# One read for both blocks of a pair, and PSUM banks split between pairs and scores, in the second layer's attentions

## The chip, the cores and the metric

The kernel runs on 1 core of a Trainium2 chip. The metric is the device time of one execution, in microseconds (us). Engines: PE is TensorE (PEld its weight loads), DVE is VectorE, ACT is ScalarE, POOL is GpSimd, SP is SyncE, which issues most DMAs.

## The reference

Two transformer layers over x (4 batches, 512 tokens, 256 features) with a context of 4 x 1601 x 192. Layer 0 has heads of 64, layer 1 has 16 heads of 16; each layer holds a self attention, a cross attention on the context and feed-forward blocks. The part that matters here is layer 1:

```python
def _attn(x, ctx, wq, wk, wv, wo, bo, num_heads):
    q = (x @ wq).reshape(B, T, num_heads, hd)      # hd = 16
    k = (ctx @ wk).reshape(B, S, num_heads, hd)
    v = (ctx @ wv).reshape(B, S, num_heads, hd)
    scores = jnp.einsum('bthd,bshd->bhts', q, k) / np.sqrt(hd)
    p = jax.nn.softmax(scores, axis=-1)
    o = jnp.einsum('bhts,bshd->bthd', p, v).reshape(B, T, E)
    return o @ wo + bo
x = _attn(_ln(x, n1_g, n1_b), _ln(x, n1_g, n1_b), sq_w, sk_w, sv_w, so_w, so_b, 16) + x
x = _ffn(_ln(x, n2_g, n2_b), f1_w1, f1_b1, f1_w2, f1_b2) + x
x = _attn(_ln(x, n3_g, n3_b), context, cq_w, ck_w, cv_w, co_w, co_b, 16) + x
x = _ffn(_ln(x, n4_g, n4_b), f2_w1, f2_b1, f2_w2, f2_b2) + x
```

## The kernel before

`build` runs five stretches one after the other. The two attentions of the second layer, `a2` (SELF1, 512 keys) and `a3` (CROSS1, 1601 keys), are both written by `attend_narrow`, each followed by its projections and feed-forward. Only that function changes.

**Groups and units.** Four heads of one batch are a group; there are 16 groups. A group's keys come in chunks of 128: 4 chunks in a2, 13 in a3. One chunk of one group is a unit, numbered tau. A group's softmax needs each query row's maximum before its exponentials, so the scores are computed twice: once in the other orientation only for the maxima, well ahead of use, and once for the exponentials.

**Steps of PE**, in the order that is written out by hand at the end of the `tensor` block (the names M, S and V are used from here on):

- M, `maxima`, L1829: one pair of matmuls, rows 0 to 62 and 64 to 126 of the array, each into one PSUM bank. An M of a2 has 512 columns, one of a3 402. A group has 8 pairs in a2 and 32 in a3 (four blocks of keys for each). DVE takes each block's row maximum with one `reduce_max` (L1965).
- S, `scores`, L1842: two matmuls (r = 0 and 1), 512 columns, each into one bank. ACT takes the exponential of each (L1920). A unit has two S, j = 0 and 1, so 4 exponentials.
- V, `values`, L1860: exponentials times values into the `pv` bank, for one half of the query columns; the first unit of a group makes one V over all 512 columns. The first V of a unit waits for all 4 exponentials of the unit before.

In a2 a unit is S M S V M V, in a3 S M V S M V, where V belongs to the unit before. `pairs_by` spreads the M over the units: two pairs in each unit of a2; in a3 three in six units of 13 and two in the others, where the third pair goes into the first half. The first group's maxima and some more (18 pairs in a2, 42 in a3) run before the first S, and the M run out before the last units: 9 units of a2 and 17 of a3 have none.

**Banks.** PSUM has 8 banks: one for `pv`, and a ring of 7 that M and S share in the order in which PE writes them (`score_place` and `item_place` number the places). Before each matmul `bank_free` waits for whoever read the bank seven places earlier: an exponential (`exp_done`) or a maximum (`item_read`):

```python
def bank_free(n):
    if n >= BANKS:
        of_maxima, m = users[n - BANKS]
        pe.wait_ge(item_read if of_maxima else exp_done, m + 1)
```

PE executes in the order of the program, so a matmul that waits holds up every step behind it.

DVE also turns a group's maxima (`turn`), the sums and their inverses (`turn_sums`, `invert_turned` in a2, `invert` in a3). ACT also copies `pv` out once a group (`raw_copy`, L1893) and casts (`high_part`, L1902).

Of the kernel before, what the change touches and what calls it, by code (L numbers as in the profile page):

```python
# [22 lines left out]
P = 128  # L23
# [1549 lines left out]
def attend_narrow(pr, name, a, block, ahead):  # L1573
# [9 lines left out]
    NI = 2 * PAIRS  # L1583
    E = 4 * NC
    BANKS = 7
# [17 lines left out]
    def unit_of(p):  # L1603
        return next(tau for tau in range(-1, T) if p < pairs_by(tau))

    def score_place(e):

        tau, j = e // 4, e % 4 // 2
        return e + 2 * (cut(tau) if j else pairs_by(tau - 1))

    unit_at = [unit_of(p) for p in range(NG * PAIRS)]

    def item_place(g):
        tau = unit_at[g // 2]
        return g + (0 if tau < 0 else 4 * tau + (2 if g // 2 < cut(tau) else 4))

    users = {score_place(e): (0, e) for e in range(4 * T)}
    users.update({item_place(g): (1, g) for g in range(2 * NG * PAIRS)})

# [4 lines left out]
    def sem(what):  # L1624
        return pr.sem(f"{name}_{what}")
# [5 lines left out]
    item_done, item_read, max_done, turned = sem("item_done"), sem("item_read"), sem("max_done"), sem("turned")  # L1631
# [12 lines left out]
    with ExitStack() as st:  # L1644
# [20 lines left out]
        def item_of(g):  # L1665

            i, m = divmod(g, NI)
            j, m = divmod(m, NI // 2)
            t, m = divmod(m, 2 * NB)
            return i, j, t, m // 2, m % 2  # L1670
# [141 lines left out]
        def _(pe):  # L1812
            def bank_free(n):

                if n >= BANKS:
                    of_maxima, m = users[n - BANKS]
                    pe.wait_ge(item_read if of_maxima else exp_done, m + 1)

            def maxima(p0, p1):
                for g in range(2 * p0, 2 * p1):  # L1820
                    i, j, t, nb, r = item_of(g)
                    if g % NI == 0:
# [6 lines left out]
                    nc.tensor.matmul(ring[:, n % BANKS, 0:a.blk], qst[i % SLOTS][rows, j, t * P:(t + 1) * P],  # L1829
                                     kst[i % SLOTS][rows, j, at:at + a.blk], start=True, stop=True)\  # L1830
                        .then_inc(item_done, 1)

            def scores(i, ch, j):
                if ch == 0 and j == 0:
                    pe.wait_ge(row_loaded[i % 2], 16 * (i // 2 + 1))
                keys = a.chunk_rows(ch)
                for r in range(2):
                    e = i * E + 4 * ch + 2 * j + r
                    n = score_place(e)
                    bank_free(n)  # L1840
                    rows = slice(64 * r, 64 * r + 64)
                    nc.tensor.matmul(ring[0:keys, n % BANKS, :], kst[i % SLOTS][rows, j, ch * P:ch * P + keys],  # L1842
                                     qst[i % SLOTS][rows, j, :], start=True, stop=True).then_inc(st_done, 1)
# [38 lines left out]
        def _(act):  # L1882
# [25 lines left out]
            for tau in range(T):  # L1908
                i, ch = divmod(tau, NC)
                if ch == 1 and i:  # L1910
                    raw_copy(i - 1)
                if tau >= HIGH_AT and (tau - HIGH_AT) % NC == 0:
                    high_part((tau - HIGH_AT) // NC)
                if tau >= RC:
                    act.wait_ge(pv_done, 2 * (tau - RC + 1))
                keys = a.chunk_rows(ch)
                for m in range(4):
                    e = 4 * tau + m
                    act.wait_ge(st_done, e + 1)
                    nc.scalar.activation(prob[0:keys, tau % RC, m, :], ring[0:keys, score_place(e) % BANKS, :],  # L1920
                                         ACT.Exp, scale=a.scale).then_inc(exp_done, 1)
# [5 lines left out]
        def _(dve):  # L1927
            def turn(i):
                dve.wait_ge(item_read, (i + 1) * NI)
# [29 lines left out]
            def blocks(g0, g1):  # L1959
                for g in range(g0, g1):  # L1960
                    i, j, t, nb, r = item_of(g)
                    c = 8 * r + 4 * j + t
                    dst = blk_max[:, i % 2, c, nb:nb + 1] if NB > 1 else row_max[:, i % 2, c:c + 1]
                    dve.wait_ge(item_done, g + 1)
                    nc.vector.reduce_max(dst, ring[:, item_place(g) % BANKS, 0:a.blk], AX.X).then_inc(item_read, 1)  # L1965
                    if g % NI == NI - 1:
                        turn(i)

            dve.wait_ge(pad_set, 1)
            blocks(0, 2 * pairs_by(-1))  # L1970
            for tau in range(T):
                if a.cross and tau >= INVERT_AT and (tau - INVERT_AT) % NC == 0:
                    invert((tau - INVERT_AT) // NC)
                blocks(2 * pairs_by(tau - 1), 2 * pairs_by(tau))
# [20 lines left out]
    return End((item_read, NG * NI), {3: (pv_copied, NG)}, stored_by)  # L1995
# [631 lines left out]
```

## Time and profile before

| | us |
|---|---|
| median of 3 runs (lowest, highest) | 3345.24 (3341.63, 3351.52) |
| the profiled execution's own time | 3350.75 |
| its span, first to last instruction | 3348.9 |
| a2: first M to last V | 2177.5 to 2379 |
| a3: first M to last V | 2635 to 3210 |

Busy shares of the whole span: PE 94%, PEld 55%, DVE 68%, ACT 54%, POOL 33%. How to read the profile: matmuls are pipelined and their ends are modelled, so a busy PE is not a PE at its peak. In a timeline, neighbouring instructions of a line are merged (x2 is two instructions), the second number is the time from the first's start to the last's end, and the bracket says how long the engine sat idle before and who released it; "issue" means nothing that the profile shows. Weight loads start when a matmul's wait has ended and so show PE's order best.

### The profile page before, as it was taken

To read this page: it belongs to the slowest core of one execution; us is meant where nothing else is said; L and a number is where in the kernel's file an instruction comes from. 1 tells how busy PE (TensorE), PEld (TensorE's weight loads), DVE (VectorE), ACT (ScalarE), POOL (GpSimd) and SP (SyncE) were. 2 spreads that over 40 slices of the span, in tenths; PEclk is the share of its full clock that TensorE was granted. 3 is DMA by queue.
4 is the path that set the end of the run, shared out by engine and by line. 5 is a ranking of instruction groups with operands and counts; after the bars stand their busy time and mean duration, and the time that the engine had idled before them with its cause. 6 is when DMAs were issued, how large, how long until landed. Compare 5 with 4: busy or idle time off the path is not lost. (4 is left out here: it accounts for less than half of the span.)

```text
span 3348.9 us, 48183 instructions
## 1 busy us (share of the span) xinstructions
PE 3159.7 (94%) x17084; PEld 1845.3 (55%) x17084; DVE 2275.3 (68%) x4098; ACT 1807.8 (54%) x3369; POOL 1088.6 (33%) x537
## 2 busy tenths in 40 slices
PE   7999997999899999999999999799898799999989
PEld 5744445788645555555555477543577544444357
DVE  5558774434567777777777555499665699999844
ACT  4445553444434444444444344368665288888864
POOL 1057770000067777777787600012100000000000
PEclk9999998999989999999999999889999699999999
DMA  6989968998976776667666423344716622323140
GB/s 233 340 230 246 239 180 312 342 333 311 311 178 141 158 164 148 149 149 166 154 149 147 162 74 139 113 139 141 265 63 231 222 75 92 106 94 104 57 148 26
DMA packets 367127, 588.80 MB, mean 176 GB/s; under 512 B 47152, under 2 KB 197216, under 8 KB 365736
## 3 DMA queue, kind: packets, MB, share of 16 engines
q1 hardware_dynamic: 361978, 582.45, 58.4%
q10 hardware_dynamic: 4910, 3.27, 0.4%
q8 instruction: 137, 2.24, 0.3%
q14 instruction: 102, 0.84, 0.1%
HBM read 344.19 MB, written 241.29 MB: 175 GB/s over the span
## 5 line engine op out<-in xcount | busy, mean ns | idle before, releaser
L2445 ACT ACTIVATE a_prob<-a_ring 128x512 f32<-128x512 f32 (+1 forms) x1088 | 552.4, 616 | 390.5 <-PE a_ring L2362 379.7
L2213 DVE TENSOR_REDUCE a_blk_max<-a_ring 128x1 f32<-128x402 f32 x992 | 502.4, 569 | 275.5 <-PE a_ring L2204 274.8
L1920 ACT ACTIVATE a_prob<-a_ring 128x512 f32<-128x512 f32 (+1 forms) x1088 | 582.3, 605 | 137.2 <-PE a_ring L1842 132.5
L2309 POOL TENSOR_TENSOR a_prob_sum<-a_prob,a_prob_sum 128x1024 f32<-128x1024 f32 x256 | 602.0, 2389 | 7.7 <-ACT a_prob L2445 7.7
L1965 DVE TENSOR_REDUCE a_blk_max<-a_ring 128x1 f32<-128x402 f32 x1024 | 506.9, 568 | 33.9 <-PE a_ring L1829 27.3
L2378 PE MATMUL a_pv<-a_prob,a_v 128*64 128x512 f32 (+1 forms) x2176 | 509.1, 607 | 0.0
L2361 PE MATMUL a_ring<-a_q_stack,a_k_stack 128*128 128x512 f32 (+1 forms) x1088 | 455.4, 419 | 12.6 <-issue 10.6
L2362 PE MATMUL a_ring<-a_q_second,a_k_second 65*128 65x512 f32 (+1 forms) x1088 | 437.3, 402 | 0.0
L2309 POOL TENSOR_TENSOR a_prob_sum<-a_prob 128x1024 f32<-128x1024 f32 x128 | 302.6, 2374 | 301.6 <-DVE a_chunk_sum L2502 200.1
L1860 PE MATMUL a_pv<-a_prob,a_v 128*32 128x256 f32 (+2 forms) x4096 | 341.5, 407 | 13.4 <-ACT a_prob L1920 7.6
L1829 PE MATMUL a_ring<-a_k_stack,a_q_stack 63*128 63x402 f32 (+1 forms) x1280 | 282.2, 423 | 39.3 <-DMA a_q_stack<-q_lo_self 18.0
L2378 PEld LDWEIGHTS a_pv<-a_prob,a_v 128*64 128x64 f32 (+1 forms) x2176 | 144.0, 138 | 271.6 <-issue 202.8
L787 DVE TENSOR_TENSOR p_split_lo<-p_ps,p_split_hi 128x402 fp32r<-128x402 f32 (+1 forms) x224 | 138.1, 622 | 217.8 <-ACT p_split_hi L708 211.7
L1842 PE MATMUL a_ring<-a_q_stack,a_k_stack 64*128 64x512 f32 (+1 forms) x1088 | 280.1, 484 | 1.0
L2361 PEld LDWEIGHTS a_ring<-a_q_stack,a_k_stack 128*128 128x128 f32 (+1 forms) x1088 | 205.9, 189 | 115.3 <-issue 60.0
L2362 PEld LDWEIGHTS a_ring<-a_q_second,a_k_second 65*128 65x128 f32 (+1 forms) x1088 | 206.9, 190 | 43.0 <-issue 0.6
L708 ACT CAST p_split_hi<-p_ps 128x402 fp32r<-128x402 f32 (+1 forms) x224 | 119.4, 534 | 205.8 <-PE p_ps L467 86.5
L1842 PEld LDWEIGHTS a_ring<-a_q_stack,a_k_stack 64*128 64x128 f32 (+1 forms) x1088 | 110.9, 182 | 210.8 <-ACT a_prob L1920 79.2
L2204 PE MATMUL a_ring<-a_k_stack,a_q_stack 64*128 64x402 f32 (+1 forms) x1224 | 208.4, 411 | 13.6 <-DMA a_q_stack<-q_hi_cross 5.5
L1799 POOL TENSOR_TENSOR a_o_full<-a_o_full,a_inv 128x512 f32<-128x512 f32 x30 | 38.5, 1284 | 562.0 <-DMA a_inv<-inverse 428.2
L1829 PEld LDWEIGHTS a_ring<-a_k_stack,a_q_stack 63*128 63x128 f32 x1280 | 145.4, 196 | 137.2 <-DVE a_row_max L1965 40.8
L2204 PEld LDWEIGHTS a_ring<-a_k_stack,a_q_stack 64*128 64x128 f32 x1224 | 95.8, 187 | 198.1 <-issue 134.0
(274 smaller groups left out, 4855.9 us busy)
## 6 DMA issues: line engine op xcount, KB each, us to landing
a_k_stack<-k_hi_cross SPq DMA_DIRECT2D x96, 400.5 KB, 4.6
a_v<-v_cross SPq DMA_DIRECT2D x48, 768.0 KB
a_k_stack<-k_lo_cross SPq DMA_DIRECT2D x80, 400.5 KB, 5.9
a_k_second<-k_hi_cross SPq DMA_DIRECT2D x32, 801.0 KB, 12.4
v_cross<-p_v_sb SPq DMA_DIRECT2D x48, 512.0 KB
k_hi_cross<-p_split_hi SPq DMA_DIRECT2D x120, 200.0 KB, 3.6
k_lo_cross<-p_split_lo SPq DMA_DIRECT2D x120, 200.0 KB, 4.7
a_q_stack<-q_hi_self SPq DMA_DIRECT2D x64, 256.0 KB, 4.3
```

Of the source, the lines that this page charges most:

```text
L1829: nc.tensor.matmul(ring[:, n % BANKS, 0:a.blk], qst[i % SLOTS][rows, j, t * P:(t + 1) * P], kst[i % SLOTS][rows, j, at:at + a.blk], start= ...
L1842: nc.tensor.matmul(ring[0:keys, n % BANKS, :], kst[i % SLOTS][rows, j, ch * P:ch * P + keys], qst[i % SLOTS][rows, j, :], start=True, stop ...
L1860: last = nc.tensor.matmul(pv[32 * h:32 * h + 32, cols], v[i % SLOTS][0:keys, ch, 32 * h:32 * h + 32], prob[0:keys, tau % RC, h, cols], sta ...
L1920: nc.scalar.activation(prob[0:keys, tau % RC, m, :], ring[0:keys, score_place(e) % BANKS, :], ACT.Exp, scale=a.scale).then_inc(exp_done, 1)
L1965: nc.vector.reduce_max(dst, ring[:, item_place(g) % BANKS, 0:a.blk], AX.X).then_inc(item_read, 1)
L2204: return nc.tensor.matmul(bank[:, 0:a.blk], qst[i % SLOTS][half, h, t * P:(t + 1) * P], kst[i % SLOTS][half, h, at:at + a.blk], start=True ...
L2213: return nc.vector.reduce_max(dst, bank[:, 0:a.blk], AX.X)
L2309: nc.gpsimd.tensor_tensor(prob_sum[:, h], prob_of(i * NCP + cp, h), other, ALU.add)\
L2361: nc.tensor.matmul(out, kst[s][:, h, k0:k0 + keys], qst[s][:, h, :], start=True, stop=False)
L2362: nc.tensor.matmul(out, k2[s][:, h, k0:k0 + keys], q2[s][:, h, :], start=False, stop=True)\
L2378: last = nc.tensor.matmul(pv[64 * h:64 * h + 64, :], v[i % SLOTS][0:keys, ch, 64 * h:64 * h + 64], prob_of(w, h)[0:keys, ch % 2, :], start ...
L2445: nc.scalar.activation(prob_of(w, h)[0:keys, ch % 2, :], ring[0:keys, score_bank(e), :], ACT.Exp, scale=a.scale).then_inc(exp_done, 1)
```

## The change

Both blocks of a pair get neighbouring banks, and one `reduce_max` over [128, 2, blk] writes both maxima. The shared ring of 7 goes: pairs have two places of two banks (4 banks), scores a ring of three banks of their own, `pv` keeps its one. The first matmul of pair p waits for the read of pair p-2 (`pair_read`); score e waits for exponential e-3 (`exp_done`). The order of PE's steps, the number of matmuls and of exponentials, LEAD, and all DMAs stay. Cut to its core:

```diff
-    BANKS = 7
+    SCORE_BANKS, PAIR_BANKS = 3, 2
...
-        ring = st.enter_context(nc.psum_tensor(f"{name}_ring", [P, BANKS, BANK], F32))
+        pairs = st.enter_context(nc.psum_tensor(f"{name}_pairs", [P, PAIR_BANKS, 2, BANK], F32))
+        ring = st.enter_context(nc.psum_tensor(f"{name}_ring", [P, SCORE_BANKS, BANK], F32))
...
             def maxima(p0, p1):
-                for g in range(2 * p0, 2 * p1):
-                    i, j, t, nb, r = item_of(g)
...
-                    n = item_place(g)
-                    bank_free(n)
-                    rows, at = slice(64 * r, 64 * r + 63), a.block_at[nb]
-                    nc.tensor.matmul(ring[:, n % BANKS, 0:a.blk], ...
+                for p in range(p0, p1):
+                    i, j, t, nb = pair_of(p)
...
+                    if p >= PAIR_BANKS:
+                        pe.wait_ge(pair_read, p - PAIR_BANKS + 1)
+                    for r in range(2):
+                        rows, at = slice(64 * r, 64 * r + 63), a.block_at[nb]
+                        nc.tensor.matmul(pairs[:, p % PAIR_BANKS, r, 0:a.blk], ...
...
             def scores(i, ch, j):
...
                 for r in range(2):
                     e = i * E + 4 * ch + 2 * j + r
-                    n = score_place(e)
-                    bank_free(n)
+                    if e >= SCORE_BANKS:
+                        pe.wait_ge(exp_done, e - SCORE_BANKS + 1)
                     rows = slice(64 * r, 64 * r + 64)
-                    nc.tensor.matmul(ring[0:keys, n % BANKS, :], ...
+                    nc.tensor.matmul(ring[0:keys, e % SCORE_BANKS, :], ...
...
-            def blocks(g0, g1):
-                for g in range(g0, g1):
-                    i, j, t, nb, r = item_of(g)
-                    c = 8 * r + 4 * j + t
-                    dst = blk_max[:, i % 2, c, nb:nb + 1] if NB > 1 else row_max[:, i % 2, c:c + 1]
-                    dve.wait_ge(item_done, g + 1)
-                    nc.vector.reduce_max(dst, ring[:, item_place(g) % BANKS, 0:a.blk], AX.X).then_inc(item_read, 1)
+            def blocks(p0, p1):
+                for p in range(p0, p1):
+                    i, j, t, nb = pair_of(p)
+                    c = slice(4 * j + t, 16, 8)
+                    dst = blk_max[:, i % 2, c, nb] if NB > 1 else row_max[:, i % 2, c]
+                    dve.wait_ge(item_done, 2 * p + 2)
+                    nc.vector.reduce_max(dst, pairs[:, p % PAIR_BANKS, :, 0:a.blk], AX.X).then_inc(pair_read, 1)
```

`turn` now waits for `pair_read`, and the phase's end counts pairs in place of blocks.

## Rows read from the trace of the kernel before

**Rows 1.** Windows: stretch, length, busy PE PEld DVE ACT POOL, PEclk, DMA, GB/s.

```profile
2198.00:2360.00 162.00, 159.33 (x1214) 63.76 (x1215) 156.46 (x278) 127.67 (x248) 30.59 (x24) 0.97 0.38 120
2779.00:3168.00 389.00, 384.38 (x3682) 157.20 (x3684) 375.19 (x780) 336.48 (x629) 29.47 (x23) 1.00 0.30 94
```

**Rows 2.** Groups of instructions, L1920, then L1965 in a3 and in a2: count, busy, mean ns.

```profile
L1920 ACT ACTIVATE a_prob<-a_ring 128x512 f32<-128x512 f32 (+1 forms) x1088 | 582.3, 605 | 137.2 <-PE a_ring L1842 132.5
...
L1965 DVE TENSOR_REDUCE a_blk_max<-a_ring 128x1 f32<-128x402 f32 x1024 | 506.9, 568 | 33.9 <-PE a_ring L1829 27.3
...
L1965 DVE TENSOR_REDUCE a_row_max<-a_ring 128x1 f32<-128x512 f32 x256 | 155.9, 676 | 22.2 <-PE a_ring L1829 22.2
```

**Rows 3.** Timeline of PEld, a3 from 2890.6: start, length, what.

```profile
2890.64 0.18 PEld L1842 LDWEIGHTS a_ring<-a_q_stack,a_k_stack 64*128 64x128 f32 x2 [0.41 <-DVE a_blk_max L1965]
...
2891.82 0.19 PEld L1842 LDWEIGHTS a_ring<-a_q_stack,a_k_stack 64*128 64x128 f32 x2 [0.41 <-issue]
...
2892.43 0.16 PEld L1860 LDWEIGHTS a_pv<-a_prob,a_v 128*32 128x32 f32 x8 [0.31 <-issue]
2893.00 0.19 PEld L1842 LDWEIGHTS a_ring<-a_q_stack,a_k_stack 64*128 64x128 f32 x2 [0.41 <-ACT a_prob L1920]
...
2893.49 0.19 PEld L1829 LDWEIGHTS a_ring<-a_k_stack,a_q_stack 63*128 63x128 f32 x2 [0.19 <-ACT a_prob L1920]
2893.87 0.16 PEld L1860 LDWEIGHTS a_pv<-a_prob,a_v 128*32 128x32 f32 x8 [0.19 <-issue]
...
2895.10 0.16 PEld L1860 LDWEIGHTS a_pv<-a_prob,a_v 128*32 128x32 f32 x8 [0.19 <-issue]
```

**Rows 4.** Timeline of ACT, a3, the same stretch.

```profile
2891.24 2.20 ACT L1920 ACTIVATE a_prob<-a_ring 128x512 f32<-128x512 f32 x4 [0.21 <-PE a_ring L1842]
```

**Rows 5.** Chain in order of time, start of a3: the first group's 64 maxima.

```profile
2635.97 31.04 DVE a_blk_max L1965 x64
```

**Rows 6.** Timeline of all engines, a3 at 2781.7, where DVE waits for an M.

```profile
2781.78 0.19 PEld L1829 LDWEIGHTS a_ring<-a_k_stack,a_q_stack 63*128 63x128 f32 x2
...
2782.39 0.58 DVE L1965 TENSOR_REDUCE a_blk_max<-a_ring 128x1 f32<-128x402 f32 x1 [0.65 <-PE a_ring L1829]
```

**Rows 7.** Timeline of PEld, a2, one group of four units.

```profile
2219.17 0.19 PEld L1842 LDWEIGHTS a_ring<-a_q_stack,a_k_stack 64*128 64x128 f32 x2 [0.41 <-ACT a_prob L1920]
...
2220.07 0.16 PEld L1860 LDWEIGHTS a_pv<-a_prob,a_v 128*32 128x32 f32 x8 [0.31 <-issue]
...
2221.64 0.19 PEld L1842 LDWEIGHTS a_ring<-a_q_stack,a_k_stack 64*128 64x128 f32 x2 [0.41 <-issue]
...
2224.79 0.26 PEld L1842 LDWEIGHTS a_ring<-a_q_stack,a_k_stack 64*128 64x128 f32 x2 [0.41 <-issue]
...
2226.06 0.18 PEld L1842 LDWEIGHTS a_ring<-a_q_stack,a_k_stack 64*128 64x128 f32 x1 [0.30 <-DVE a_row_max L1965]
2226.48 0.16 PEld L1860 LDWEIGHTS a_pv<-a_prob,a_v 128*32 128x32 f32 x8 [0.24 <-issue]
2227.48 0.19 PEld L1829 LDWEIGHTS a_ring<-a_k_stack,a_q_stack 63*128 63x128 f32 x2 [0.84 <-DVE a_row_max L1965]
2227.59 0.19 PEld L1842 LDWEIGHTS a_ring<-a_q_stack,a_k_stack 64*128 64x128 f32 x2
...
2230.74 0.18 PEld L1842 LDWEIGHTS a_ring<-a_q_stack,a_k_stack 64*128 64x128 f32 x2 [0.41 <-ACT a_prob L1920]
```

**Rows 8.** Timeline of ACT, a2, the exponentials of units one, three and four.

```profile
2219.76 2.07 ACT L1920 ACTIVATE a_prob<-a_ring 128x512 f32<-128x512 f32 x4 [0.95 <-PE a_ring L1842]
...
2225.41 2.07 ACT L1920 ACTIVATE a_prob<-a_ring 128x512 f32<-128x512 f32 x4
...
2228.31 2.06 ACT L1920 ACTIVATE a_prob<-a_ring 128x512 f32<-128x512 f32 x4 [0.33 <-PE a_ring L1842]
```

**Rows 9.** Timeline of PEld, a2: first S of the first and last unit without M.

```profile
2358.08 0.30 PEld L1842 LDWEIGHTS a_ring<-a_q_stack,a_k_stack 64*128 64x128 f32 x4 [0.41 <-ACT a_prob L1920]
...
2375.03 0.30 PEld L1842 LDWEIGHTS a_ring<-a_q_stack,a_k_stack 64*128 64x128 f32 x4 [0.41 <-ACT a_prob L1920]
```

More of the change, by code:

```diff
@@ L1601, in cut @@
         return (pairs_by(tau - 1) + pairs_by(tau) + 1) // 2
[L1603 to L1618, printed above, removed]
     def by_turns(i):
@@ L1630, in attend_narrow @@
     pad_set = sem("pad_set")
[L1631 removed]
+    item_done, pair_read, max_done, turned = sem("item_done"), sem("pair_read"), sem("max_done"), sem("turned")
     max_stored, row_loaded = ([sem(f"{what}{n}") for n in range(2)] for what in ("max_stored", "row_loaded"))
@@ L1661, in attend_narrow, with pair_of @@
         den = sb("den", [P, OS, 16])
-        ring = st.enter_context(nc.psum_tensor(f"{name}_ring", [P, BANKS, BANK], F32))
+        pairs = st.enter_context(nc.psum_tensor(f"{name}_pairs", [P, PAIR_BANKS, 2, BANK], F32))
+        ring = st.enter_context(nc.psum_tensor(f"{name}_ring", [P, SCORE_BANKS, BANK], F32))
         pv = st.enter_context(nc.psum_tensor(f"{name}_pv", [P, BANK], F32))
[L1665 to L1670, printed above, removed]
+        def pair_of(p):
+            i, m = divmod(p, PAIRS)
+            j, m = divmod(m, PAIRS // 2)
+            return i, j, m // NB, m % NB
         @block.sync
@@ L1825, in maxima @@
                             pe.wait_ge(filled[i], 32)
-                    n = item_place(g)
-                    bank_free(n)
-                    rows, at = slice(64 * r, 64 * r + 63), a.block_at[nb]
-                    nc.tensor.matmul(ring[:, n % BANKS, 0:a.blk], qst[i % SLOTS][rows, j, t * P:(t + 1) * P],
-                                     kst[i % SLOTS][rows, j, at:at + a.blk], start=True, stop=True)\
-                        .then_inc(item_done, 1)
+                    if p >= PAIR_BANKS:
+                        pe.wait_ge(pair_read, p - PAIR_BANKS + 1)
+                    for r in range(2):
+                        rows, at = slice(64 * r, 64 * r + 63), a.block_at[nb]
+                        nc.tensor.matmul(pairs[:, p % PAIR_BANKS, r, 0:a.blk], qst[i % SLOTS][rows, j, t * P:(t + 1) * P],
+                                         kst[i % SLOTS][rows, j, at:at + a.blk], start=True, stop=True)\
+                            .then_inc(item_done, 1)
             def scores(i, ch, j):
@@ L1838, in scores @@
                     e = i * E + 4 * ch + 2 * j + r
-                    n = score_place(e)
-                    bank_free(n)
+                    if e >= SCORE_BANKS:
+                        pe.wait_ge(exp_done, e - SCORE_BANKS + 1)
                     rows = slice(64 * r, 64 * r + 64)
-                    nc.tensor.matmul(ring[0:keys, n % BANKS, :], kst[i % SLOTS][rows, j, ch * P:ch * P + keys],
+                    nc.tensor.matmul(ring[0:keys, e % SCORE_BANKS, :], kst[i % SLOTS][rows, j, ch * P:ch * P + keys],
                                      qst[i % SLOTS][rows, j, :], start=True, stop=True).then_inc(st_done, 1)
@@ L1919, in _ @@
                     act.wait_ge(st_done, e + 1)
-                    nc.scalar.activation(prob[0:keys, tau % RC, m, :], ring[0:keys, score_place(e) % BANKS, :],
+                    nc.scalar.activation(prob[0:keys, tau % RC, m, :], ring[0:keys, e % SCORE_BANKS, :],
                                          ACT.Exp, scale=a.scale).then_inc(exp_done, 1)
@@ L1928, in turn @@
             def turn(i):
-                dve.wait_ge(item_read, (i + 1) * NI)
+                dve.wait_ge(pair_read, (i + 1) * PAIRS)
                 if NB > 1:
@@ L1973, in _ @@
                     invert((tau - INVERT_AT) // NC)
-                blocks(2 * pairs_by(tau - 1), 2 * pairs_by(tau))
+                blocks(pairs_by(tau - 1), pairs_by(tau))
                 if not a.cross and tau >= TURN_AT and (tau - TURN_AT) % NC == 0:
@@ L1994, in attend_narrow @@
     pr.end_join()
-    return End((item_read, NG * NI), {3: (pv_copied, NG)}, stored_by)
+    return End((pair_read, NG * PAIRS), {3: (pv_copied, NG)}, stored_by)
 def attend_then_feed(pr, attend, names, a, **feed):
```

11 lines of the change are left out of this document (3 added, 8 removed).

## The prediction

> **What bounds the kernel now.** I read the windows of the two attentions first, then the groups of instructions for the price of a read, then the timelines of PE's weight loads and of ACT, which show who waits for whom.
>
> By the windows DVE is busy 156.46 of 162 us in a2 and 375.19 of 389 in a3, and PE as long [rows 1]: two engines look full, and shares can't say which one sets the pace. The timeline of a3 can. From one S to the next with one M and one V between it takes 1.18 us, twice running (2890.64, 2891.82, 2893.00); the V before the last S is released by nothing ("issue") and the S follows it by 0.57 [rows 3]. So in the halves with one pair PE runs its own chain without waiting. Waits stand in the halves with two pairs: the second M, 2893.49, is released by ACT, 0.05 after the last of four exponentials ended (2891.24 + 2.20 = 2893.44) [rows 3, 4]. That 0.05 is the price of a semaphore below. So a3 is PE's, with DVE just behind it.
>
> a2 is another case. Its four units take 2.47, 3.15, 2.80 and 3.15 us [rows 7]. In the first nothing waits. In the others M, or the second matmul of the second S, is released by a read of DVE, as 2226.06 shows [rows 7]. There DVE does set the pace.
>
> **The reads.** A read of 402 columns takes 0.568, one of 512 0.676 [rows 2]: 0.98 ns a column. 64 in a row take 31.04, so 0.485 each [rows 5]; less 402 columns (0.395) that leaves 0.09 that a joined read saves. A pair's read in a3 should then last 0.568 + 0.395 = 0.96, one every 0.88 in place of 0.97. No row shows a read over two banks. Bounds: it costs two reads (1.14, nothing saved), or it saves the whole 0.17 that a read holds beyond its columns. I take 0.09, since the run of 64 is the nearest row. Over 640 pairs that is 58 us of DVE; what of it reaches the end is the question.
>
> **a2, the scores' ring.** Here is the step that I think decides. In a2 the order is S M S V M V. The fourth score of a unit now waits for the exponential of the unit's first one (e-3), so PE, at the second S, stands until ACT has it, with V, M, V and the next unit queued behind. Before, this matmul waited for a read of the unit before, or for nothing. An exponential lasts 0.60 [rows 2]; with the semaphore 0.65 from its start. The first exponential starts 0.59 after its S in the first unit (2219.76 - 2219.17), 0.62 in the third, 0.72 in the fourth [rows 7, 8]; I take 0.60 for the second, whose form is the first's. Then V follows the late matmul by 0.42 (2226.06 to 2226.48), and the next S follows V by 1.57 (2220.07 to 2221.64) [rows 7]:
>
> - first unit: 0.59 + 0.65 + 0.42 + 1.57 = 3.23, before 2.47: +0.76
> - second: 3.24, before 3.15: +0.09
> - third: its late matmul already came at 2226.06 = 2225.41 + 0.65, so the exponential binds as soon as the read did: 0
> - fourth: 3.36, before 3.15: +0.21
>
> A group goes from 11.57 to 12.63, +1.06. A joined read of 2 x 512 columns comes about every 1.1 (2 x (0.485 + 110 x 0.00098) less 0.09), two a unit: 2.2 of 3.2, and a group's turns fit in the rest. So the reads leave the path and the M no longer wait. From 2219.17 to 2358.08 there are 12 such groups [rows 7, 9], and the four units before 2219.17 have the same form: 13 x 1.06 = **+13.8**.
>
> **a2, its ends.** Without M a unit takes (2375.03 - 2358.08)/8 = 2.12 [rows 9]. The new loop is 0.59 + 0.65 + 0.42, then V, V, S: 1.57 less the M's step of 0.57 is 1.00. That makes 2.66, +0.54 for eight units, **+4.3**. The 18 pairs at the start are read at DVE's pace, except while a load is awaited: **-1**.
>
> **a3, the scores' ring.** A V stands between the two S, so the loop is longer. The second matmul of a second S needs the exponential of the first score of the S before: 2891.24 + 0.65 = 2891.89, where S came at 2891.82 [rows 3, 4]. It waits 0.07, and the M and V behind it. At the first S of the next unit the needed exponential starts about 2 x 0.49 + 0.13 later than 2891.24 (0.49 is the step of the four in 2.07, 0.13 the surplus of 2.20 [rows 4, 8]), 2892.35 + 0.65 = 2893.00, the very moment: nothing. So 0.07 in each unit with two pairs, seven a group: +0.5. After a half with two pairs there is none, PE being late anyway.
>
> **a3, the pairs' places.** In a half with two pairs the second M needs the read of the pair before the last. M's weights to the start of its read: 0.61 (2781.78 to 2782.39) [rows 6]; read 0.96; semaphore 0.05: 1.62. That M comes 0.11 after its S (the step between neighbours, 2227.48 to 2227.59 [rows 7]), so 1.07 before the S in question: the second M is free 0.55 after S, before 0.49; V follows by 0.38 (2893.49 to 2893.87) [rows 3], 0.06 later than now. In the next half M waits for the first of the two: 0.11 + 0.61 + 0.96 + 0.05 = 1.73 after the first S, V 0.38 on is 2.11, now 2.10 (2893.00 to 2895.10) [rows 3]. Even. What the old ring made PE wait there for exponentials the pairs' places make it wait for reads. The turn of the maxima on DVE no longer reaches PE, since two pairs are ahead: I allow -0.1 a group. Sum +0.4 a group, (512 - 42) pairs by 32 = 14.7 groups: **+6**. The start, 42 pairs at DVE's pace: 42 x 0.09 = **-3.8**. The last 17 units wait for all exponentials of a unit at V, later than the ring's waits: 0.
>
> **The sum.** 13.8 + 4.3 - 1 + 6 - 3.8 = +19.3, on 3350.75, the profiled execution's own time (span 3348.9): 3370. That execution lies 5.5 above the median of the runs, 3345.24, so against medians I say 3365.
>
> **The rivals.**
>
> *DVE is the bound in both, and the joined read pays* (faster). For it: 96% busy in both [rows 1]. Place: every M that waits for a read; price 0.09 for each of 640 pairs, 58 us, 3288. It decides if M's release by DVE, and not PE's own chain or an exponential, ends last in most halves of a3; the 1.18 that repeats with "issue" speaks against it [rows 3]. The Trainium skill (Perfetto Trace Analysis, Optimizing Scalar/DVE Operations) gives about 125 ns of overhead for a DVE access to PSUM, and says grouping helps if the engine is saturated; the run of 64 reads shows 0.09, and by the page's figure this rival would be 80 us, an estimate. Chance 0.08.
>
> *The places suffice, a2 stays DVE's* (no change). Place: the fourth score of a2's units. If ACT releases it 0.35 earlier than I reckon (1.06 over the three units that grow), nothing is lost there, and DVE goes on setting the pace with joined reads: less 8 x 0.09 a group, of which the two pairs read ahead of the V over 512 columns give nothing, so 0.54 x 13 = 7. With a3's +6 and -3.8 and a2's start that is -6: 3339. Against it: the third unit, where the exponential comes at the very time of the read. Chance 0.10.
>
> *The pair's read costs two reads* (the change doesn't do what it says). Then each second M in a3 comes 0.18 later, and the M after it as well: 0.36 at most for six units, of which I take half for slack: 1.1 a group, +16, and the gains at the starts go, +5: 3386. Chance 0.10.
>
> **How the numbers follow.** The forecast, chance 0.72, is 3365, by itself 3354 to 3376: down 11 if a3's +6 and the tail's 4.3 vanish, up 11 if the joined read saves about half of what I take. About 0.3%, 10 us, is what a measurement of this kernel can tell from no change. Faster: the first rival and a fifth of the second, 0.10. Within 0.3%: the rest of the second and a shade of the forecast's low end, 0.10. Slower: the forecast and the third rival, 0.80. The range reaches up to the third rival and down past the forecast's own low end, leaving out the first rival and most of the second: 3346 to 3386.
>
> **What would show it.** In the changed profile, in a2: the second matmul of the second S released by ACT in every unit, units of 3.2 to 3.4 and groups of 12.6; DVE idle for about 1 us a unit before its reads, released by PE. Units near 2.12 with no M would show the ring's price wrong. In a3: groups longer by 0 to 0.8 us, the 0.07 at a second S, reads of 0.96 and a lower busy share of DVE. If a3's groups get shorter by 0.9 or more, PE's chain was not the bound and the first rival holds. If reads last 1.1 or more, the third does.

## The result, and the profile after

The changed kernel takes 3374.74 us (median of 4 runs, 3372.66 to 3379.22); beside it the kernel before takes 3348.38 (4 runs, 3341.63 to 3352.75). The ratio is 1.0090, 95% interval 1.0068 to 1.0111: slower by 23 to 37 us. The profiled execution took 3372.66 itself, its span is 3370.8.

**By stage.** The stretch ahead of a2, which the change doesn't touch, ends between 2161.8 and 2178.3 in the traces of this study, so spans of single executions can't be compared to better than 16 us. Their stages can, as far as they repeat. Each time below is the distance between the starts of two matmuls in the PE timeline: the first M to the first S ("start"), the units with M, the units without, up to the next stage's first matmul. In a2 the first five units stand apart.

| us | before | after | difference | forecast |
|---|---|---|---|---|
| a2 start | 19.9 | 21.0 | +1.1 | -1 |
| a2 units 1 to 5 | 16.66 | 21.71 | +5.1 | in the next |
| a2 units 6 to 55 | 144.07 | 158.51 | +14.4 | +13.8 |
| a2 units without M, last V | 21.4 | 25.1 | +3.7 | +4.3 |
| a3 start | 39.2 | 38.4 | -0.8 | -3.8 |
| a3 the 191 units with M | 493.0 | 505.2 | +12.2 | +6 |
| a3 units without M | 42.1 | 44.4 | +2.3 | 0 |

The forecast of 4.3 is for eight of a2's nine units without M; those eight take 16.95 and 21.42, +4.5. How well a stage repeats, from the traces of all the runs below: with the code of before a2's units 6 to 55 take 143.99 to 144.10 (seven traces), and a3's 191 units 493.0, 493.4 and 495.3; with the changed code the 191 units take 505.2, 505.9 and 506.1.

**The reads** first: the groups of instructions of the kernel after (count, busy, mean ns of one, idle ahead of them and who ended it), then the chain of waits at the start of a3 (start, length, what).

```profile
L1942 DVE TENSOR_REDUCE a_blk_max<-a_pairs 128x2 f32<-128x804 f32 x512 | 485.3, 992 | 65.5 <-PE a_pairs L1806 61.8
L1942 DVE TENSOR_REDUCE a_row_max<-a_pairs 128x2 f32<-128x1024 f32 x128 | 152.9, 1217 | 45.4 <-PE a_pairs L1806 43.0
...
L1806 PEld LDWEIGHTS a_pairs<-a_k_stack,a_q_stack 63*128 63x128 f32 x1280 | 135.3, 197 | 141.1 <-DVE a_blk_max L1942 56.2 <-DVE a_row_max L1942 27.0 <-issue 18.5
L1819 PEld LDWEIGHTS a_ring<-a_q_stack,a_k_stack 64*128 64x128 f32 (+1 forms) x1088 | 125.3, 184 | 257.6 <-ACT a_prob L1897 200.7 <-issue 53.3
```

```profile
2643.60 29.24 DVE a_blk_max L1942 x32
```

One read over two banks works: 32 pairs take 29.24, 0.914 each, where 64 single reads took 31.04, 0.970 a pair [rows 5]. It saves 0.056 a pair, not the 0.09 forecast, and lasts 0.992, not 0.96. In a2 (DVE timelines of before and after) 16 single reads take 9.66, eight of pairs 9.15:

```profile
2178.38 9.66 DVE L1965 TENSOR_REDUCE a_row_max<-a_ring 128x1 f32<-128x512 f32 x16 [17.15 <-PE a_ring L1829]
...
2162.78 9.15 DVE L1942 TENSOR_REDUCE a_row_max<-a_pairs 128x2 f32<-128x1024 f32 x8 [16.97 <-PE a_pairs L1806]
```

Of the groups the last is the one to see: the scores' loads now wait for exponentials for 200.7 us in all, 79.2 before.

**a2.** PEld timeline of the kernel after, one group of four units, beside [rows 7] of before; ACT in the same stretch, beside [rows 8].

```profile
2217.43 0.19 PEld L1819 LDWEIGHTS a_ring<-a_q_stack,a_k_stack 64*128 64x128 f32 x2 [0.41 <-issue]
...
2218.71 0.18 PEld L1819 LDWEIGHTS a_ring<-a_q_stack,a_k_stack 64*128 64x128 f32 x1 [0.75 <-ACT a_prob L1897]
2219.14 0.16 PEld L1837 LDWEIGHTS a_pv<-a_prob,a_v 128*32 128x32 f32 x8 [0.25 <-issue]
...
2220.24 0.19 PEld L1819 LDWEIGHTS a_ring<-a_q_stack,a_k_stack 64*128 64x128 f32 x2
...
2221.62 0.18 PEld L1819 LDWEIGHTS a_ring<-a_q_stack,a_k_stack 64*128 64x128 f32 x1 [0.71 <-ACT a_prob L1897]
...
2223.61 0.19 PEld L1819 LDWEIGHTS a_ring<-a_q_stack,a_k_stack 64*128 64x128 f32 x2 [0.41 <-issue]
...
2224.86 0.18 PEld L1819 LDWEIGHTS a_ring<-a_q_stack,a_k_stack 64*128 64x128 f32 x1 [0.71 <-ACT a_prob L1897]
...
2226.85 0.19 PEld L1819 LDWEIGHTS a_ring<-a_q_stack,a_k_stack 64*128 64x128 f32 x2 [0.41 <-issue]
...
2230.08 0.19 PEld L1819 LDWEIGHTS a_ring<-a_q_stack,a_k_stack 64*128 64x128 f32 x2 [0.41 <-issue]
```

```profile
2224.21 2.07 ACT L1897 ACTIVATE a_prob<-a_ring 128x512 f32<-128x512 f32 x4 [1.17 <-PE a_ring L1819]
2227.45 2.07 ACT L1897 ACTIVATE a_prob<-a_ring 128x512 f32<-128x512 f32 x4 [1.17 <-PE a_ring L1819]
```

Units (S to S) take 2.81, 3.37, 3.24 and 3.23, the group 12.65. In each the fourth score comes last, released by ACT 1.24 to 1.38 after the unit's first S. ACT starts its first exponential 0.60 after that S (2223.61, 2224.21), the score follows 0.65 later (2224.86), and V, M, V behind it put the next S off to 2226.85. ACT then idles for 1.17, so in such a unit each engine waits once for the other. The same ring without any M, PEld timeline, first and last unit; then PE's waits of the stretch 2205 to 2363 (what waits for whom: us in all, times, longest).

```profile
2363.03 0.29 PEld L1819 LDWEIGHTS a_ring<-a_q_stack,a_k_stack 64*128 64x128 f32 x3 [0.41 <-issue]
2364.28 0.18 PEld L1819 LDWEIGHTS a_ring<-a_q_stack,a_k_stack 64*128 64x128 f32 x1 [0.95 <-ACT a_prob L1897]
...
2384.46 0.29 PEld L1819 LDWEIGHTS a_ring<-a_q_stack,a_k_stack 64*128 64x128 f32 x3 [0.41 <-ACT a_prob L1897]
```

```profile
PEld a_ring L1819 <- ACT a_prob L1897: 36.3, 50, 1.0
...
PEld a_pairs L1806 <- DVE a_row_max L1942: 10.9, 13, 0.8
```

(2384.46 - 2363.03)/8 = 2.68 a unit, 2.12 before [rows 9]. PE waits for an exponential 50 times in some 50 units, and for a read only 13 times: once a group.

**a3.** PEld timeline, a half with two pairs and the two after it, beside [rows 3]; then the window of the units with M (length, busy PE, PEld, DVE, ACT, POOL, PEclk, DMA, GB/s), beside [rows 1].

```profile
2933.37 0.19 PEld L1819 LDWEIGHTS a_ring<-a_q_stack,a_k_stack 64*128 64x128 f32 x2 [0.41 <-ACT a_prob L1897]
2933.48 0.19 PEld L1806 LDWEIGHTS a_pairs<-a_k_stack,a_q_stack 63*128 63x128 f32 x2
2933.96 0.19 PEld L1806 LDWEIGHTS a_pairs<-a_k_stack,a_q_stack 63*128 63x128 f32 x2 [0.29 <-DVE a_blk_max L1942]
2934.34 0.16 PEld L1837 LDWEIGHTS a_pv<-a_prob,a_v 128*32 128x32 f32 x8 [0.19 <-issue]
2934.91 0.18 PEld L1819 LDWEIGHTS a_ring<-a_q_stack,a_k_stack 64*128 64x128 f32 x2 [0.41 <-ACT a_prob L1897]
...
2935.55 0.16 PEld L1837 LDWEIGHTS a_pv<-a_prob,a_v 128*32 128x32 f32 x8 [0.19 <-issue]
2936.12 0.18 PEld L1819 LDWEIGHTS a_ring<-a_q_stack,a_k_stack 64*128 64x128 f32 x2 [0.41 <-ACT a_prob L1897]
...
2937.31 0.24 PEld L1819 LDWEIGHTS a_ring<-a_q_stack,a_k_stack 64*128 64x128 f32 x2 [0.41 <-ACT a_prob L1897]
...
2937.99 0.16 PEld L1837 LDWEIGHTS a_pv<-a_prob,a_v 128*32 128x32 f32 x8 [0.32 <-issue]
2938.56 0.19 PEld L1819 LDWEIGHTS a_ring<-a_q_stack,a_k_stack 64*128 64x128 f32 x2 [0.41 <-ACT a_prob L1897]
```

```profile
2693.00:3182.00 489.00, 481.17 (x4512) 196.15 (x4504) 441.15 (x499) 411.29 (x769) 34.63 (x27) 1.00 0.29 89
```

The second M is released by the read of the pair before the last, 0.59 after S; V follows S by 0.97, before by 0.87 [rows 3]. In the unit behind, V follows the second S by 0.68 (2937.31 to 2937.99), before by 0.61 [rows 3]. Both the new waits of the forecast are there. DVE's share fell from 0.965 to 0.90, and the stretch got longer all the same.

A unit falls into two halves, from one S to the next. Their lengths over all 191 units, from the first weight loads of each S in the PEld timelines, show where the loop grew by 12.5 (12.2 by matmul starts). The 88 halves with two pairs take 8.5 us more in all (15 of them, behind a group's V over 512 columns, 2.0 of it). The 88 second halves of the units with two pairs, one M in each half, take 5.6 more. All others together take 1.7 less.

### The profile page after: what moved, and what is told of

Its sections match the earlier page's. It is cut to its first block and busy times, and to the rows that moved or that the text cites. A ratio compares the mean times of both kernels' runs of the same rounds, so it can differ in the third digit from the quotient of the medians.

```text
span 3370.8 us, 47541 instructions
## 1 busy us (share of the span) xinstructions
PE 3165.3 (94%) x17084; PEld 1834.3 (54%) x17084; DVE 2241.6 (66%) x3458; ACT 1809.4 (54%) x3369; POOL 1090.2 (32%) x537
## 3 DMA queue, kind: packets, MB, share of 16 engines
q8 instruction: 137, 2.24, 0.3%
## 5 line engine op out<-in xcount | busy, mean ns | idle before, releaser
L2190 DVE TENSOR_REDUCE a_blk_max<-a_ring 128x1 f32<-128x402 f32 x992 | 502.4, 570 | 272.6 <-PE a_ring L2181 271.9
L1942 DVE TENSOR_REDUCE a_blk_max<-a_pairs 128x2 f32<-128x804 f32 x512 | 485.3, 992 | 65.5 <-PE a_pairs L1806 61.8
L2338 PE MATMUL a_ring<-a_q_stack,a_k_stack 128*128 128x512 f32 (+1 forms) x1088 | 455.1, 418 | 12.2 <-issue 10.3
L1819 PE MATMUL a_ring<-a_q_stack,a_k_stack 64*128 64x512 f32 (+1 forms) x1088 | 312.7, 492 | 23.3 <-ACT a_prob L1897 23.3
L1806 PE MATMUL a_pairs<-a_k_stack,a_q_stack 63*128 63x402 f32 (+1 forms) x1280 | 274.9, 422 | 48.6 <-DMA a_q_stack<-q_lo_cross 16.6
L1819 PEld LDWEIGHTS a_ring<-a_q_stack,a_k_stack 64*128 64x128 f32 (+1 forms) x1088 | 125.3, 184 | 257.6 <-ACT a_prob L1897 200.7
L1806 PEld LDWEIGHTS a_pairs<-a_k_stack,a_q_stack 63*128 63x128 f32 x1280 | 135.3, 197 | 141.1 <-DVE a_blk_max L1942 56.2
```

Source lines behind the costliest of these rows:

```text
L1806: nc.tensor.matmul(pairs[:, p % PAIR_BANKS, r, 0:a.blk], qst[i % SLOTS][rows, j, t * P:(t + 1) * P], kst[i % SLOTS][rows, j, at:at + a.blk ...
L1819: nc.tensor.matmul(ring[0:keys, e % SCORE_BANKS, :], kst[i % SLOTS][rows, j, ch * P:ch * P + keys], qst[i % SLOTS][rows, j, :], start=True ...
L1942: nc.vector.reduce_max(dst, pairs[:, p % PAIR_BANKS, :, 0:a.blk], AX.X).then_inc(pair_read, 1)
L2190: return nc.vector.reduce_max(dst, bank[:, 0:a.blk], AX.X)
L2338: nc.tensor.matmul(out, kst[s][:, h, k0:k0 + keys], qst[s][:, h, :], start=True, stop=False)
```

## The experiments

Stages are read as above. Several kernels have an attention of the changed kernel beside one of before, and line numbers differ. Each stage is read from one execution.

**One attention at a time.** The changed `attend_narrow` in a2 with the old one, here named `attend_cross`, in a3, and the other way round.

```diff
-attend_then_feed(pr, attend_narrow, ("a3", ...
+attend_then_feed(pr, attend_cross, ("a3", ...
```

> The change in a2 alone; a3 as before. Ring theory (a2's fourth score waits for the exponential of its unit's first score): a2 from its first M to the end of its last V 226 us as in the changed kernel (202 before), groups of 12.65, units without M 2.67; a3 574 as before; in all +24 us on the kernel before. Rival, DVE's joined reads or the neighbouring banks are what costs: the loss goes with the number of joined reads, of which a2 has 128 of 640, so about a fifth of the changed kernel's +26, +5 us.

> The change in a3 alone; a2 as before. Theory: a3's groups 34.3 us as in the changed kernel (33.4 before), 14.7 of them +13.8, less 1 to 2 at its start: +13 us on the kernel before, a2 202 as before. Rival, the cost goes with the reads: 512 of 640, +21 us. Rival, DVE was the bound in a3: faster, 512 x 0.053 = 27 us.

Measured: a2 alone 3362.72 against 3343.06, ratio 1.0062 (1.0043 to 1.0082), so +14 to +27 us; a3 alone 3353.84, 1.0034 (1.0017 to 1.0051), +6 to +17. By stages, a2 alone: units 6 to 55 158.23 (+14.2), eight units without M 21.42 (+4.5), start +1.9; a2 in all 221.9, where 226 was expected from the one trace of the changed kernel. a3 alone: start -0.8, units with M 505.9 (+12.9). Both parts cost, a2 more. In this second execution a2's first five units took 16.71, as before, and in the a3-only one a3's units without M 40.9: the +5.1 and most of the +2.3 in the table go with the granted clock of that one execution (see the end), and don't come back with the change. Without them the table's sum of +38.0 is +30.6; the ratio has +30, the medians +26.

**The order of a2.** V between the two S, as a3 has it, which leaves a V's time more before the fourth score:

```diff
-                if tau and a.cross:
+                if tau:
                     values(tau - 1, 0)
                 scores(i, ch, 1)
-                if tau and not a.cross:
-                    values(tau - 1, 0)
```

> The changed kernel with a2's first V put between its two S, as a3 has it; same instructions, same banks. Ring theory: the exponential of the unit's first score then has a V and an M to hide behind; DVE's two joined reads (1.13 each) and a turn set a2's pace, 2.75 to 2.9 a unit, groups 11.0 to 11.6 against 12.65, units without M 2.24 against 2.67: a2 203 to 208 in place of 226, a3 588 unchanged, 18 to 23 us faster than the changed kernel. Rival, joined reads or neighbouring banks slow a2: no change, a2 226.

Measured: 3347.06, ratio 1.0016 (1.0001 to 1.0032), so about 25 less than the change by the two ratios, 28 by the medians. a2 takes 201.3, below the 203 to 208 expected, and a3's units with M 506.1, unchanged. a2's units 6 to 55 take 140.62, 2.81 a unit. PEld timeline of this kernel, a2: two S without a wait of their second matmul, and the fourth score behind a group's full V, which still waits.

```profile
2243.14 0.19 PEld L1819 LDWEIGHTS a_ring<-a_q_stack,a_k_stack 64*128 64x128 f32 x2 [0.41 <-ACT a_prob L1895]
...
2244.38 0.19 PEld L1819 LDWEIGHTS a_ring<-a_q_stack,a_k_stack 64*128 64x128 f32 x2 [0.41 <-ACT a_prob L1895]
...
2249.05 0.19 PEld L1806 LDWEIGHTS a_pairs<-a_k_stack,a_q_stack 63*128 63x128 f32 x2 [0.74 <-DVE a_row_max L1940]
...
2251.66 0.18 PEld L1819 LDWEIGHTS a_ring<-a_q_stack,a_k_stack 64*128 64x128 f32 x1 [0.65 <-ACT a_prob L1895]
```

One step moved takes 17.9 of the 158.5 away and leaves a2's loop 3.5 shorter than before. So in the changed kernel the loop of score, exponential and score set a2's pace, not the reads. The units without M stay dear: 2.54 each (20.28 for eight, 16.95 before), where 2.24 was expected.

**The same order in the kernel before**, as a control for how much of those 3.5 the joined read gave.

> The kernel before with nothing changed but the order: in a2 the first V between the two S. Theory: there DVE sets the pace with single reads, so the order gains little: a2 groups 11.3 to 11.6, a2 199 to 203, the time the same within 3 us. Rival, the order is a gain of its own of the size seen in the changed kernel: 18 us faster.

Measured: 3340.30, ratio 0.9997 (0.9985 to 1.0008). Units 6 to 55 take 140.76, the units without M 2.9 more than before. The order gives the loop 3.3, and its price at the end gives that back. With this order the loop is as long with the old reads and banks as with the new. What holds it is not the same: in this kernel DVE is busy for 139.4 of the 140.8 us and PE's loads wait for reads 48 times, in the changed one with this order DVE is busy for 135.5 of 140.6, and the loads wait for exponentials 75 times and for reads 12 times. So this pair of runs shows that reads and banks together give a2 nothing, and not what joined reads alone would give. No run has joined reads with a ring of seven.

**Two reads again, in the same places.**

```diff
+                    for r in range(2):
-                    dve.wait_ge(item_done, 2 * p + 2)
+                        dve.wait_ge(item_done, 2 * p + r + 1)
-                    nc.vector.reduce_max(dst, pairs[:, p % PAIR_BANKS, :, 0:a.blk], AX.X).then_inc(pair_read, 1)
+                        last = nc.vector.reduce_max(dst, pairs[:, p % PAIR_BANKS, r, 0:a.blk], AX.X)
+                    last.then_inc(pair_read, 1)
```

> The changed kernel with two reads for a pair again, one for each bank, in the same banks and with the same waits of PE. Theory (DVE off the path in a2, its read's end on the path in a3's halves with two pairs): a2 226 to 227; a3's second M and the M after it released 0.06 later (1.05 in place of 0.99 after the read's start), 0.06 to 0.12 for each of six units, +0.4 to +0.7 a group, with the start +8 to +12 in all. Rival, DVE sets the pace of both: 128 x 0.064 + 512 x 0.053 = +35 us. Rival, the joined read itself costs: faster.

Measured: 3380.43, ratio 1.0119 (1.0096 to 1.0141) to before, over the change by some 6 by the medians and 10 by the two ratios, whose intervals overlap. a2's units 6 to 55 take 158.23, as with the joined read; a3's start 40.6 (+2.2), its units with M 508.1 (+2.0 to 2.9). Under this layout the joined read saves 5 by these stages, less than the 8 to 12 expected; the whole times don't settle it. The split of the banks alone so costs about 40 by the ratio, and the joined read gives back a small part. The split read can start behind the first of the two matmuls, which may be why so little is lost; that was not tried apart.

**Which wait makes a3 longer?** Reads over half their columns in a3, in the changed a3 and in that of before (a2 as before in both). Before's edit is the same cut on its own read.

```diff
-nc.vector.reduce_max(dst, pairs[:, p % PAIR_BANKS, :, 0:a.blk], AX.X)
+nc.vector.reduce_max(dst, pairs[:, p % PAIR_BANKS, :, 0:a.blk // 2], AX.X)
```

> a2 as before, a3 as changed, with every read of the third attention over only the first 201 of a block's 402 columns (the maxima of the other columns are left out). It divides the 12 us by which the third attention's 191 units with M are longer after the change (493.4 before, 505.2 to 506.1 after) between the two waits that I name: the pairs' places and the scores' ring. A pair's read gets shorter by about 402 x 0.00098 = 0.39 us, 0.99 to 0.60, so no M should wait for a place. Theory (half of the 12 is the places' wait, half the ring's): 505.9 goes to 498 to 500, and the longest waits of PE left are those of the scores for exponentials. Rival A (the ring alone): it stays within 2 of 505.9. Rival B (the places alone): 492 to 495. The same cut in the kernel before stands beside it as control.

> Control: the kernel before with the same cut in the third attention (each read over 201 of 402 columns, the other columns' maxima left out). In the kernel before, M and S wait for reads in turn within one ring of seven. If PE's own chain and the exponentials set the pace there, the 191 units stay within 2 of 493.4; if DVE, 96% busy, set it, they fall by 20 or more.

The groups of the two kernels' reads, the changed one first:

```profile
L2367 DVE TENSOR_REDUCE a_blk_max<-a_pairs 128x2 f32<-128x402 f32 x512 | 285.7, 576 | 236.7 <-PE a_pairs L2231 234.8
```

```profile
L2390 DVE TENSOR_REDUCE a_blk_max<-a_ring 128x1 f32<-128x201 f32 x1024 | 317.1, 360 | 200.6 <-PE a_ring L2254 197.5
```

Measured: units with M 488.1 in the changed a3 (505.9 with whole reads), 489.4 in that of before (493.0). The cut takes 17.8 off the changed a3 and 3.6 off the old one, more than even rival B had it (492 to 495), and more than the 2 expected of the control. With short reads the two are alike, the changed one shorter by 1.3, less than the old one differs from trace to trace. By this total alone the whole +12.9 would lie in the waits for the pairs' places; the halves, below, say otherwise. The control also settles the share of DVE: 37% off its reads' busy time in a3 (506.9 [rows 2] to 317.1) moved the old a3's units with M by 0.7%. The PEld timeline of the changed a3 with short reads, the second half of a unit with two pairs, then a half with two pairs:

```profile
2909.18 0.24 PEld L2244 LDWEIGHTS a_ring<-a_q_stack,a_k_stack 64*128 64x128 f32 x2 [0.41 <-issue]
...
2909.86 0.16 PEld L2262 LDWEIGHTS a_pv<-a_prob,a_v 128*32 128x32 f32 x8 [0.33 <-issue]
2910.43 0.19 PEld L2244 LDWEIGHTS a_ring<-a_q_stack,a_k_stack 64*128 64x128 f32 x2 [0.41 <-ACT a_prob L2322]
2910.53 0.42 PEld L2231 LDWEIGHTS a_pairs<-a_k_stack,a_q_stack 63*128 63x128 f32 x4
2911.22 0.16 PEld L2262 LDWEIGHTS a_pv<-a_prob,a_v 128*32 128x32 f32 x8 [0.26 <-issue]
2911.79 0.19 PEld L2244 LDWEIGHTS a_ring<-a_q_stack,a_k_stack 64*128 64x128 f32 x2 [0.41 <-ACT a_prob L2322]
```

The four matmuls of two pairs run on (x4), V follows S by 0.79 in place of 0.97. But in the half ahead of it V still follows S by 0.68 (2909.18 to 2909.86): that wait is not for a read.

**The same for the exponentials**, over half their columns, in both; the other half of the probabilities is set to 1 once.

```diff
-nc.scalar.activation(prob[0:keys, tau % RC, m, :], ring[0:keys, e % SCORE_BANKS, :],
+nc.scalar.activation(prob[0:keys, tau % RC, m, 0:HALF], ring[0:keys, e % SCORE_BANKS, 0:HALF],
```

> a2 as before, a3 as changed, with every exponential of the third attention over 256 of its 512 columns (the other probabilities are set to 1 once and left). It takes the ring's waits away instead: an exponential falls from 0.60 by some 0.2 us or more. Theory (half of the 12 is the ring's): 505.9 goes to 498 to 500, and what is left over the control is the places', 5 to 7. Rival A (the ring alone): within 2 of the control. Rival B (the places alone): it stays 10 or more above the control.

> Control: the kernel before with the same cut of the exponentials in the third attention (256 of 512 columns). There the second M of a unit's half with two pairs waits for an exponential, about 0.24 us beyond PE's own chain in each of some seven halves a group; shorter exponentials should free part of it: 493.4 goes to 480 to 491.

Measured: exponentials last 0.381 in place of 0.60 in both. Units with M 500.7 in the changed a3 (-5.2), 481.7 in that of before (-11.3), so the changed one is 19.0 longer where it had been 12.9. The old a3 was held more by exponentials, the changed one more by reads. The PEld timeline of the changed a3 with short exponentials, the second half of a unit with two pairs:

```profile
2909.72 0.19 PEld L2245 LDWEIGHTS a_ring<-a_q_stack,a_k_stack 64*128 64x128 f32 x2 [0.41 <-ACT a_prob L2324]
...
2910.33 0.16 PEld L2263 LDWEIGHTS a_pv<-a_prob,a_v 128*32 128x32 f32 x8 [0.31 <-issue]
2910.90 0.19 PEld L2245 LDWEIGHTS a_ring<-a_q_stack,a_k_stack 64*128 64x128 f32 x2 [0.41 <-ACT a_prob L2324]
```

V follows this S by 0.61 again. The totals of both cuts speak for rival B, the places alone. The halves don't. Their mean lengths, from the same weight loads, the changed a3 in the a3-only run (the 73 halves with two pairs that are not behind a V over 512 columns; the 88 second halves of units with two pairs):

| us | halves with two pairs | second halves of units with two pairs |
|---|---|---|
| a3 of before | 1.453 | 1.176 |
| changed a3 | 1.542 | 1.238 |
| changed, short reads | 1.367 | 1.267 |
| before, short reads | 1.440 | 1.176 |
| changed, short exponentials | 1.573 | 1.177 |
| before, short exponentials | 1.388 | 1.175 |

The growth of the halves with two pairs goes with the reads, so it is the places'. That of the second halves stays when the reads are short and goes when the exponentials are: it is the ring's. The totals hid it, since each cut also takes away what was there before the change: the halves with two pairs of the old a3 wait for exponentials (1.453 to 1.388), and with short reads those of the changed a3 fall below even the old ones.

**Spreading the maxima.** If the two pairs in one half are the cause, three pairs of a unit in three gaps should cost nothing. a2 as before, a3 changed, and in units with three pairs:

```diff
                 scores(i, ch, 0)
-                maxima(pairs_by(tau - 1), cut(tau))
+                maxima(p0, min(p0 + 1, p1))
                 values(tau - 1, 0)
+                if third:
+                    maxima(p0 + 1, p0 + 2)
                 scores(i, ch, 1)
-                maxima(cut(tau), pairs_by(tau))
+                if not third:
+                    maxima(min(p0 + 1, p1), p1)
                 values(tau - 1, 1)
+                if third:
+                    maxima(p0 + 2, p1)
```

> a2 as before. a3 as changed, but in units with three pairs the second M stands before the second S and the third behind the last V, so that each M comes over 1.1 us after the one before it; same instructions and banks. Theory (in a3 the M wait for the read of the pair before the last, some 1.65 us after that pair's weights, because two M stand together): a unit with three pairs and the one after it take 4.9 together against 5.18 in the changed kernel and 5.04 before; six a group, 14.7 groups: a3 from its first S to the end of its M 481 to 488 in place of 505.5 (493 to 495 before), 20 us faster than the change in a3 alone. Rival, the waits for exponentials by the ring of three are what costs in a3: 505 unchanged, since each half then still meets them. Rival, the joined reads or the banks cost: unchanged.

Measured: 3334.59 against 3340.78, ratio 0.9982 (0.9968 to 0.9996). a3's units with M take 489.4: 16.5 less than in the changed a3 alone, nearly what the short reads gave, and 3.6 less than before. It missed the 481 to 488 expected by little; that the ring of three alone had made a3 longer is ruled out, since the ring is the same here. PEld timeline of this kernel: a unit with three pairs and the S of the next.

```profile
2919.87 0.19 PEld L2244 LDWEIGHTS a_ring<-a_q_stack,a_k_stack 64*128 64x128 f32 x2 [0.41 <-ACT a_prob L2327]
2919.97 0.19 PEld L2231 LDWEIGHTS a_pairs<-a_k_stack,a_q_stack 63*128 63x128 f32 x2
2920.48 0.16 PEld L2262 LDWEIGHTS a_pv<-a_prob,a_v 128*32 128x32 f32 x8 [0.31 <-ACT a_prob L2327]
2921.05 0.19 PEld L2231 LDWEIGHTS a_pairs<-a_k_stack,a_q_stack 63*128 63x128 f32 x2 [0.41 <-issue]
...
2921.65 0.16 PEld L2262 LDWEIGHTS a_pv<-a_prob,a_v 128*32 128x32 f32 x8 [0.31 <-issue]
2922.22 0.19 PEld L2231 LDWEIGHTS a_pairs<-a_k_stack,a_q_stack 63*128 63x128 f32 x2 [0.41 <-DVE a_blk_max L2372]
2922.33 0.26 PEld L2244 LDWEIGHTS a_ring<-a_q_stack,a_k_stack 64*128 64x128 f32 x2
```

The three M stand 1.08 and 1.17 apart, and the unit takes 2.46; in the changed kernel one with three pairs took 2.75 (1.54 + 1.21, 2933.37 to 2936.12).

**Both mended.** a3 as in the last; a2 changed, with V between the S while there are M, and for the units without M the old order and all seven banks for scores (short of the function that picks the bank):

```diff
+                if tau and 4 * tau < TAIL:
+                    values(tau - 1, 0)
                 scores(i, ch, 1)
-                if tau and not a.cross:
+                if tau and 4 * tau >= TAIL:
                     values(tau - 1, 0)
```

> The a3 of the run with spread pairs, and an a2 with joined reads, its first V between the two S as long as there are M, and all seven banks for scores and the old order once there are none. Theory: a2 197 to 200 (201 with the order alone; units without M back at 2.12), a3 as in the run with spread pairs, so 15 to 20 us faster than the kernel before. If the spread does nothing: a2's 3 us faster alone, and 11 slower in a3.

Measured: 3334.80 against 3340.78, ratio 0.9977 (0.9961 to 0.9994). By stages a2 takes 197.9 (202.0 before), a3 568.3 (574.3). Both this and the last beat the kernel before, by some 6 us, 0.2% (1 to 11 and 2 to 13), and with the same median: the 4 us of a2 are seen in the trace alone. The 15 to 20 expected of this kernel were missed; its two stages show 10.

## Why the prediction was right, and where its sum was short

It gave 3365, in 3346 to 3386, and slower at 0.80; the kernel takes 3374.74 and is slower by 0.9%. The mechanism was right and the sum too small: +19.3 forecast, +30 by the ratio, +26 by the medians. Against the stages' 30.6 the sum lacks 11.3: 6.2 in a3's loop, 5.1 in the two starts.

- **a2, the scores' ring: right.** The group quoted begins with the forecast's third unit: 2.81, 3.37, 3.24, 3.23 where 2.80, 3.36, 3.23, 3.24 were forecast, 12.65 for 12.63. Over 50 units that made +14.2 to 14.4, where 13.3 was meant for them (12.5 groups by 1.06). The order's experiment shows the cause: the fourth score behind the unit's first exponential. That DVE set the pace here before is right but for the order: with one V moved the loop is 3.3 shorter, and the old reads keep DVE busy for 139.4 of its 140.8 us.
- **A joined read's saving: 0.09 forecast, 0.056 measured.** The 0.09 mixed two kinds of rows. 0.98 ns a column is how the mean length of a read grows from 402 to 512 columns; 0.485 is the step of reads in a row. By steps alone (9.66 for 16 reads over 512 columns, 0.604 each, against 0.485) a column is 1.08 ns, and 0.485 less 402 of them leaves 0.05.
- **a2, the ends: right, but for the start.** A unit without M takes 2.68 where 2.66 was forecast. The start got longer by 1 to 2 where -1 was forecast. I had overlooked how far M runs ahead of the reads: seven banks are 3.5 pairs, two places are 2. Before the last of 18 pairs can be written, before needs 36 - 7 = 29 reads, after 16 pairs, 32 reads: 3 x 0.60 more, less 16 x 0.064 saved, +0.8. Before's code shows 19.6 to 21.1 there in this study, so no more than the direction is shown.
- **a3, the start: wrong.** "42 x 0.09 = -3.8" measured -0.8. The same slip: 84 - 7 = 77 single reads before, 80 in 40 pairs after, +3 x 0.485, less 40 x 0.056 = -0.8.
- **a3, the pairs' places: the term that was mis-sized.** The forecast had V 0.06 later in a half with two pairs, "Even" in the next half, -0.1 for the turn: about nothing, and it gave its +0.4 a group to the scores' ring. V came 0.10 later in the half quoted, the half behind gave 0.02 back, and a group took 0.83 more (12.2 / 14.7). Over the 191 units all halves but the ring's take 6.8 more. The read lasts 0.992, not 0.96, and the M stands 0.59 after S, not 0.55. Behind a group's full V, M waits for a place once more (0.32 at 2928.82 in the trace), which I had left out.
- **a3, the scores' ring: right, a little large.** V follows the second S by 0.68 (2937.31 to 2937.99), 0.07 more than the 0.61 of before [rows 3], as forecast, and short exponentials take it away. It makes 5.6 us, where seven units a group gave 0.5 x 14.7 = 7.4; six of the seven have it, not the one with the V over 512 columns.
- **a3 before the change: not only PE's own chain.** "a3 is PE's, with DVE just behind it" holds for DVE (short reads gave 3.6), but short exponentials took 11.3 off the old loop. The exponentials, more than DVE, stood behind PE.
- **a3, the units without M: right.** They take 40.85 to 40.88 with either code, in every trace whose granted clock there was 1.00 and whose exponentials were whole.
- **The rivals.** That DVE is the bound fell: its busy share fell and the time rose, and 37% less reading moved the old a3's loop by 3.6. That a2 stays DVE's fell with the 50 waits for ACT. That a pair's read costs two reads fell with 0.914 against 0.970. The Trainium skill (Perfetto Trace Analysis, Optimizing Scalar/DVE Operations) puts about 125 ns of overhead on a DVE access to PSUM. The joined read saves 56 ns over 402 columns here, less than half of it, so the measurement decides. Reads in a row overlap: single ones last 0.568 and come every 0.485.

## What to carry to other kernels

Splitting a shared ring changes how far the writer may run ahead of each reader, and that is priced at the place where two writes to one ring stand closest in program order: here a unit's fourth score, with one M between it and the first S and let through only 1.24 to 1.38 behind that S, and a second M 0.1 behind an S and the first M. An engine at 96% can be off the path: look for a chain that repeats, and shorten the suspect's work in both kernels before paying for it. Such a probe also removes waits that the change didn't make, so read it at the place of the wait and not by the loop's total: the totals gave a3's whole loss to the places, the halves give 5.6 of 12.5 to the ring. When a ring has to be smaller, spread the writes over the gaps of the order that are there; it gave back 16 us here, and moving one V 18.

## What the runs showed that I had not expected

- The joined read saves little: 0.056 a pair over 402 columns, and 0.064 over 512.
- The stretch ahead of a2, with the same code, ended from 2161.8 to 2178.3 over the traces of this study. Its cause was not looked for.
- PE's clock rose late in one execution. The window of the changed kernel behind a2's first S, then the one that follows:

```profile
2182.40:2204.50 22.10, 21.97 (x98) 8.60 (x98) 13.97 (x14) 10.58 (x20) 0.00 (x0) 0.50 0.29 86
2205.00:2363.00 158.00, 143.68 (x1096) 56.28 (x1094) 137.80 (x148) 115.47 (x225) 30.68 (x24) 1.00 0.35 111
```

The granted clock was 0.50, the lower level (1.2 GHz), for 22 us after the start in which PE had waited for reads. Over the first five units its mean was 0.71 in the kernel before and 0.77 in the a2-only run, whose a2 is the same as here. The five units took 21.71, in those two 16.66 and 16.71: 5 us that a comparison of two single traces would have laid to the change. a3's units without M are alike: 44.4 here at a mean of 0.88, 42.1 in the kernel before at 0.96, and 40.9 in the a3-only run at 1.00.
